# Running sums of a rotated attention trace from rounded high and low parts, with the context scaling moved to ScalarE

## What is computed

```python
v = x @ Wv.T
rotors = exp(1j * t[:, None] * freqs[None, :])
memory_trace = cumsum(v * rotors, axis=1)
retrieved = real(memory_trace * conj(rotors))
x = layernorm(x + retrieved @ Wo.T)

s = einsum('bsd,btd->bst', x, ctx) / 16 * Dm         # Dm: normalised decay, lower triangle
v = maximum(abs(sum(s, axis=-1)), 1.0)
x = layernorm(x + einsum('bst,btd->bsd', s / v[:, None, :], ctx))

logits = x @ router_w.T                               # top 2 of 8 experts, then the experts
x = layernorm(x + sum_e gate_e * (silu(x @ up_e) * (x @ up_e')) @ down_e)
```

## Time and profile before

| | us |
|---|---|
| median of three runs | 265.36 (264.54 to 266.08) |
| the profiled execution, own time | 262.09 |
| its span, first to last instruction | 260.3 |

### The profile page before, as it was taken

How to read it: one execution, slowest core, us unless ns; L and a number is a source line. 1 busy time by engine, 2 the same in 40 slices (tenths; PEclk the granted TensorE clock), 3 DMA queues, 4 the chain that set the end, 5 groups by cost and what they waited for, 6 DMA issues and landing times.

```text
span 260.3 us, 5161 instructions
## 1 busy us (share of the span) xinstructions
PE 206.9 (79%) x1365; PEld 181.5 (70%) x1366; DVE 162.7 (62%) x534; ACT 111.1 (43%) x277; POOL 143.0 (55%) x132
## 2 busy tenths in 40 slices
PE   8669899999999997756999999999999999300000
PEld 8557798898888996745888888888888888200000
DVE  5856888888887684954554544554545454118992
ACT  2323144244234113641454545454545454425665
POOL 0074674674675310565577777777777774416340
PEclk9999999999999999979999999999999999955555
DMA  7964665765641012802222323233232341089323
GB/s 217 383 260 149 239 188 197 231 229 184 225 122 43 0 44 89 276 3 60 81 89 92 101 86 101 89 99 101 85 101 89 102 91 66 9 271 317 139 90 151
DMA packets 20129, 35.73 MB, mean 137 GB/s; under 512 B 2861, under 2 KB 11312, under 8 KB 20112
## 3 DMA queue, kind: packets, MB, share of 16 engines
q1 hardware_dynamic: 16368, 26.21, 30.0%
q0 software_dynamic: 3744, 9.31, 11.8%
HBM read 27.12 MB, written 9.31 MB: 140 GB/s over the span
## 4 chain that ended last, share of the span: by engine, by line
PE 65%; DVE 17%; issue 6%; POOL 4%; DMA 4%; ACT 2%; SPq 1%; DVEq 0%; ACTq 0%; POOLq 0%
PE p_c L545 14%; PE p_v L545 7%; PE p_y L467 6%; PE p_v L411 4%; PE p_y L571 4%; PE p_r L545 4%; PE p_a L545 3%; PE p_s L545 3%; PE p_t L584 3%; PE p_s L451 3%; POOL space L992 3%; PE p_c L427 3%; DVE space L838 3%; PE p_r L495 2%; PE p_a L486 2%
## 5 line engine op out<-in xcount | busy, mean ns | idle before, releaser
L545 PE MATMUL p_c<-w_hi,parts 128*128 x104 | 34.7, 414 | 0.0
L1016 POOL DMA_INDIRECT y_dram<-x1T,scatter_now x26 | 26.3, 1013 | 11.8 <-issue 6.2
L996 POOL DMA_INDIRECT turns<-x_dram,gather_now x26 | 25.4, 979 | 12.6 <-issue 3.8
L983 POOL TENSOR_TENSOR w_lo<-keep,w_hi 128x1536 fp32r<-128x1536 f32 (+1 forms) x8 | 27.5, 3440 | 0.0
L810 DVE TENSOR_TENSOR parts<-p_y,parts 128x256 fp32r<-128x256 f32 x39 | 16.5, 424 | 17.4 <-ACT parts L912 17.4
L820 DVE TENSOR_TENSOR cs<-p_c,cs 128x256 f32<-128x256 f32 x26 | 11.0, 424 | 22.8 <-ACT cs L919 22.8
L970 POOL TENSOR_TENSOR space<-back 128x512 f32<-128x512 f32 x8 | 10.1, 1267 | 26.9 <-DVE back L704 26.9
L919 ACT ACTIVATE cs<-p_c 128x256 f32<-128x256 f32 x26 | 10.1, 387 | 24.8 <-PE p_c L545 24.8
L978 POOL TENSOR_TENSOR cs<-space,vinv 128x256 f32<-128x256 f32 x16 | 9.5, 613 | 18.3 <-DVE vinv L718 14.9
L545 PEld LDWEIGHTS p_c<-w_hi,parts 128*128 128x128 f32 x104 | 17.6, 189 | 2.4
L912 ACT ACTIVATE parts<-p_y 128x256 fp32r<-128x256 f32 x39 | 14.9, 381 | 8.6 <-PE p_y L571 8.5
(11 more groups left out here) (153 smaller groups left out, 551.4 us busy)
## 6 DMA issues: line engine op xcount, KB each, us to landing
keep<-in_weights SPq DMA_DIRECT2D x8, 768.0 KB, 4.4
space<-y_dram SPq DMA_DIRECT2D x16, 256.0 KB, 4.1
space<-in_xT SPq DMA_DIRECT2D x8, 256.0 KB, 3.5
keep<-in_x SPq DMA_DIRECT2D x8, 256.0 KB, 3.6
space<-in_ctxT SPq DMA_DIRECT2D x8, 256.0 KB, 2.8
space<-in_ctxt SPq DMA_DIRECT2D x8, 256.0 KB, 3.0
x_dram<-x SPq DMA_DIRECT2D x8, 256.0 KB, 2.2
keep<-x_dram SPq DMA_DIRECT2D x1, 2048.0 KB, 8.4
```

Of the source, the lines that this page charges most:

```text
L545: last = nc.tensor.matmul(dst, lhs[:, k, :], w[:].rearrange("p e n -> p (e n)")[:, bass.ds(start + col + k * width, width)], start=(n == 0 ...
L983: nc.gpsimd.tensor_tensor(w_lo[:, bass.ds(i, 1), :].rearrange("p a n -> p (a n)"), w_in[s], w_hi[:, bass.ds(i, 1), :].rearrange("p a n -> ...
L996: nc.gpsimd.indirect_dma_start(xs[s], None, x2_dram, bass.IndirectOffsetOnAxis(ap=gather_now[s][:], axis=0)).then_inc(xs_ok[s], 16)
L1016: nc.gpsimd.indirect_dma_start(y_dram, bass.IndirectOffsetOnAxis(ap=scatter_now[s][:], axis=0), ys[s], None, bounds_check=TOPK * N - 1, oo ...
```

## The change

Four things. (1) `turned` is split into `turned_hi`, its value rounded by ACT (two copies of 512 columns a pair), and `turned_lo`, the rest, subtracted by POOL (two of 512 columns); `tri` is copied once into the rounded `tri_exact`; the sums are now sixteen float32r matmuls, high and low part of each block adding into the same place of `p_c`. PE waits for the low part of each sequence by itself. (2) The context rows are no longer scaled; instead ACT scales `att` by `vinv` into `att_div` (two of 128 columns), and PE multiplies `att_div` by `c_in` directly. (3) ACT's `w_hi` stands right behind `sd1` instead of behind `vabs`, and POOL's `w_lo` is cut into four quarters of 384 columns, the first ahead of `got` and three behind it. (4) SP's load of the next context rows waits for the `p_a` matmuls, and its last read-back waits for `w_lo`.

```diff
--- before.py
+++ after.py
@@ -141,6 +141,7 @@
         att = sb("att", [P, 2, T])
+        att_div = sb("att_div", [P, 2, T])
@@ -161,6 +162,9 @@
         parts = sb("parts", [P, 4 * RING, KC, P], F32R)
+        turned_hi, turned_lo = (parts[:].rearrange("p a k t -> p (a k t)")[:, n * 4 * D:(n + 1) * 4 * D].rearrange(
+            "p (q h d) -> p q h d", q=2, h=2) for n in range(2))
+        tri_exact = sb("tri_exact", [P, P], F32R)
         shift = [sb(f"shift{s}", [P, 2]) for s in range(2)]
@@ -275,6 +279,7 @@
         eps_ok = sem("eps_ok")
+        tri_ok, turned_hi_ok, turned_lo_ok = (sem(n) for n in ("tri_ok", "turned_hi_ok", "turned_lo_ok"))
         v_ok, turned_ok, sums_ok, back_ok, got_ok, y_ok = (sem(n) for n in (
@@ -351,7 +356,7 @@
                     if has(-1):
-                        sp.wait_ge(cs_ok, i)
+                        sp.wait_ge(av_ok, i)
                     load(c_in, ctxt, c_ok, i + 1, 1 - s)
@@ -369,6 +374,8 @@
 
+            sp.wait_ge(lo_ok, PAIRS)
+
             sp.dma_start(x2_keep.rearrange("p j n -> p (j n)").rearrange("p (j q d) -> p (j q) d", q=2, d=D),
@@ -420,13 +427,16 @@
                 if has(0):
-                    pe.wait_ge(turned_ok, i + 1)
-                    for q in range(2):
+                    if isinstance(i, int) and i == 0:
+                        pe.wait_ge(tri_ok, 1)
+                    for q in range(2):
+                        pe.wait_ge(turned_lo_ok, 2 * i + q + 1)
                         for h in range(2):
                             for k in range(KC):
-                                last = nc.tensor.matmul(p_c[:, q, h, k * T:(k + 1) * T],
-                                                        turned[:, q, h, k * P:(k + 1) * P], tri,
-                                                        start=True, stop=True)
+                                for n, share in enumerate((turned_hi, turned_lo)):
+                                    last = nc.tensor.matmul(p_c[:, q, h, k * T:(k + 1) * T],
+                                                            share[:, q, h, k * P:(k + 1) * P], tri_exact[:],
+                                                            start=(n == 0), stop=(n == 1))
                     last.then_inc(sums_ok, 1)
@@ -438,7 +448,7 @@
                     if has(0):
-                        pe.wait_ge(turned_ok, i + 1)
+                        pe.wait_ge(turned_ok, 2 * i + 2)
                     values(0, xT_in[1 - s])
@@ -479,11 +489,12 @@
                     keep_busy(idle[3], ident, 0)
+                    pe.wait_ge(c_ok[1 - s], 8 * (i - 1 - (1 - s)) + 16)
                     pe.wait_ge(cs_ok, i)
...
                     for q in range(2):
-                        last = nc.tensor.matmul(p_a[:, q, :], att[:, q, :], cs[:, q, :], start=True, stop=True)
+                        last = nc.tensor.matmul(p_a[:, q, :], att_div[:, q, :], c_in[1 - s][:, q, :], start=True, stop=True)
                     last.then_inc(av_ok, 1)
@@ -654,10 +665,12 @@
                 dve.wait_ge(v_ok, j + 1)
+                if not (isinstance(j, int) and j == 0):
+                    dve.wait_ge(turned_lo_ok, 2 * j)
                 for q in range(2):
-                    last = nc.vector.tensor_tensor(
-                        turned[:, q, :, :], p_v[:, q:q + 1, :].to_broadcast([P, 2, D]), rotor[:, 0, :, :], ALU.mult)
-                last.then_inc(turned_ok, 1)
+                    nc.vector.tensor_tensor(
+                        turned[:, q, :, :], p_v[:, q:q + 1, :].to_broadcast([P, 2, D]), rotor[:, 0, :, :],
+                        ALU.mult).then_inc(turned_ok, 1)
 
@@ -867,23 +880,38 @@
             act.wait_ge(eps_ok, 1)
+            act.wait_ge(const_in, 16)
+            nc.scalar.activation(tri_exact[:], tri, ACT.Copy).then_inc(tri_ok, 1)
 
...
                     nc.scalar.activation(sd1[:], mv1[:, :, 1], ACT.Sqrt, bias=eps[:]).then_inc(sd1_ok, 1)
-                    act.wait_ge(t1_ok, i)
-                    nc.scalar.activation(x1T[:], p_t[:], ACT.Copy).then_inc(x1T_ok, 1)
-                if has(-2):
-                    act.wait_ge(mv2_ok, 2 * i - 2)
-                    nc.scalar.activation(sd2[:], mv2[:, :, 1], ACT.Sqrt, bias=eps[:]).then_inc(sd2_ok, 1)
-                if has(-1):
-                    act.wait_ge(sum_ok, i)
-                    nc.scalar.activation(vabs[:], rowsum, ACT.Abs).then_inc(vabs_ok, 1)
                 if has(0):
...
                                          ACT.Copy).then_inc(hi_ok, 1)
+                if has(-1):
+                    act.wait_ge(t1_ok, i)
+                    nc.scalar.activation(x1T[:], p_t[:], ACT.Copy).then_inc(x1T_ok, 1)
+                if has(-2):
+                    act.wait_ge(mv2_ok, 2 * i - 2)
+                    nc.scalar.activation(sd2[:], mv2[:, :, 1], ACT.Sqrt, bias=eps[:]).then_inc(sd2_ok, 1)
+                if has(-1):
+                    act.wait_ge(sum_ok, i)
+                    nc.scalar.activation(vabs[:], rowsum, ACT.Abs).then_inc(vabs_ok, 1)
+                    act.wait_ge(vinv_ok, i)
+                    if has(-2):
+                        act.wait_ge(av_ok, i - 1)
+                    for q in range(2):
+                        last = nc.scalar.activation(att_div[:, q, :], att[:, q, :], ACT.Copy, scale=vinv[:, q:q + 1])
+                    last.then_inc(cs_ok, 1)
+                if has(1):
+                    if has(0):
+                        act.wait_ge(sums_ok, i + 1)
+                    for q in range(2):
+                        act.wait_ge(turned_ok, 2 * i + 3 + q)
+                        nc.scalar.activation(turned_hi[:, q, :, :], turned[:, q, :, :], ACT.Copy).then_inc(turned_hi_ok, 1)
                 if has(-2):
@@ -962,28 +990,30 @@
 
+            def low_part(e, s, quarter):
+
+                n = slice(quarter * W_END // 4, (quarter + 1) * W_END // 4)
+                whole = w_hi[:, bass.ds(e, 1), :].rearrange("p a n -> p (a n)")
+                return nc.gpsimd.tensor_tensor(w_lo[:, bass.ds(e, 1), :].rearrange("p a n -> p (a n)")[:, n], w_in[s][:, n],
+                                               whole[:, n].bitcast(F32), ALU.subtract)
+
             def step(i, s, has):
                 if has(0):
+                    pool.wait_ge(hi_ok, i + 1)
+                    low_part(i, s, 0)
                     pool.wait_ge(back_ok, i + 1)
...
                                             back[:, :, 1, :].rearrange("p q (k t) -> p q k t", k=KC), ALU.add).then_inc(got_ok, 1)
-                if has(-1):
-                    pool.wait_ge(c_ok[1 - s], 8 * (i - 1 - (1 - s)) + 16)
-                    pool.wait_ge(vinv_ok, i)
-                    if has(-2):
-                        pool.wait_ge(av_ok, i - 1)
-                    for q in range(2):
-                        last = nc.gpsimd.tensor_tensor(cs[:, q, :], c_in[1 - s][:, q, :], vinv[:, q:q + 1].to_broadcast([P, D]), ALU.mult)
-                    last.then_inc(cs_ok, 1)
-
-                if has(0):
-                    pool.wait_ge(hi_ok, i + 1)
-                    nc.gpsimd.tensor_tensor(w_lo[:, bass.ds(i, 1), :].rearrange("p a n -> p (a n)"), w_in[s],
-                                            w_hi[:, bass.ds(i, 1), :].rearrange("p a n -> p (a n)").bitcast(F32),
-                                            ALU.subtract).then_inc(lo_ok, 1)
-
+                    for quarter in range(1, 4):
+                        last = low_part(i, s, quarter)
+                    last.then_inc(lo_ok, 1)
+                if has(1):
+                    for q in range(2):
+                        pool.wait_ge(turned_hi_ok, 2 * i + 3 + q)
+                        nc.gpsimd.tensor_tensor(turned_lo[:, q, :, :], turned[:, q, :, :],
+                                                turned_hi[:, q, :, :].bitcast(F32), ALU.subtract).then_inc(turned_lo_ok, 1)
             pipeline(pool, step)
```

More of the change, by code:

```diff
@@ L874, in step @@
                     nc.scalar.activation(sd1[:], mv1[:, :, 1], ACT.Sqrt, bias=eps[:]).then_inc(sd1_ok, 1)
+                if has(0):
+                    act.wait_ge(w_ok[s], 8 * (i - s) + 16)
+                    nc.scalar.activation(w_hi[:, bass.ds(i, 1), :].rearrange("p a n -> p (a n)"), w_in[s],
+                                         ACT.Copy).then_inc(hi_ok, 1)
+                if has(-1):
                     act.wait_ge(t1_ok, i)
@@ L882, in step @@
                     nc.scalar.activation(vabs[:], rowsum, ACT.Abs).then_inc(vabs_ok, 1)
-                if has(0):
-                    act.wait_ge(w_ok[s], 8 * (i - s) + 16)
-                    nc.scalar.activation(w_hi[:, bass.ds(i, 1), :].rearrange("p a n -> p (a n)"), w_in[s],
-                                         ACT.Copy).then_inc(hi_ok, 1)
+                    act.wait_ge(vinv_ok, i)
[5 more added lines that the diff above has]
+                if has(1):
+                    if has(0):
+                        act.wait_ge(sums_ok, i + 1)
+                    for q in range(2):
```

(2 more changed lines are left out.)

1 line of the change is left out of this document (removed).

## The result

The changed kernel takes **279.15 us** (277.99 to 280.55, four runs) against 264.95 for the kernel before in the same runs: ratio **1.057 [1.052, 1.063]**, 14.2 us slower. The forecast was 275.8, with a range of 270.5 to 281.5.

What follows compares the result with a forecast made beforehand. PE was taken to bound the middle, at about 9.65 us a step, and a chain of waits the start. Start +6.05, pair 1 +0.2, middle +4.5 and end -0.3 made +10.45: 275.8 us, range 270.5 to 281.5.

Steps and rivals of the forecast that it cites:

- The sign: Whole kernel: the change makes it slower, chance 0.96, against faster 0.03 and same 0.01.
- the sums: Sums on PE: sixteen rounded matmuls take 1.76 to 1.95 us in place of 1.89, nothing won or lost.
- the start: Pair 0: ACT rounds only behind its last Sin, then PE runs the sums at half clock, turn back at 17.9, +6.05.
- The rival in which they halve and PE keeps that: Sums on PE: they halve, saving 0.94 us in seven steps, total change -3.0, 262.4 us; chance 0.04.
- The 0.5 given back a step later: After pair 1's transposes: one step on, x1 is no longer under POOL's long w_lo, so 0.5 us returns.
- The middle: Steps 2 to 6: POOL's quarters hold DVE's x2, so x2T is late and PE stalls, 0.9 a step, +4.5.
- The step that failed: Middle, x2's normalisation: only the second quarter precedes the second L651, x2 at 53.5 instead of 52.87, vinv at 53.9.
- POOL runs all three quarters through: Middle: DVE gets in only after all three quarters, x2 at 54.6, 1.85 a step, +15.2, 280.5 us; chance 0.08.
- 0.15 a step for `att_div`: Middle, ACT: att_div at 0.4 us each pushes the rounding by 0.15, counted within the 0.9 a step.
- The rest costs nothing there: Middle: other moved work, such as w_hi ahead of x1T, POOL's subtractions and SP's context load, adds 0.
- The end: End of the stage: L682 is no longer slowed from 0.26 to 0.64 us by POOL's context scaling, -0.3.
- holding 0.2 to 1.85 a step: Middle: bounds on the loss per step from POOL's quarters holding DVE, 0.2 without holding, 1.85 with all three run through.

Runs made afterwards that it cites:

- the low part placed: Changed kernel with w_lo in two pieces, 640 columns behind vinv and 896 behind x1 of the next step: 267.45 us, ratio 1.0132.
- the placed scaling: Kernel before with only context scaling moved to ACT, w_hi at the start of the step and whole w_lo behind vinv: 261.73 us, ratio 0.9928.
- everything placed: Changed kernel with w_lo cut at column 640 into gaps, pair 0 rounded early, 24 idle matmuls at the start, x2T between the roundings: 264.83 us, ratio 1.0082.

## Why the prediction was right, and where it was not

**The sign, the sums and the start: right.** The sums came at 1.85 us (chain, 70.92), within 1.76 to 1.95, and the run with sixteen rounded matmuls shows the term of 0 by itself. The rival in which they halve and PE keeps that is refuted twice: sixteen take as long as before, and with eight, which do take half as long, the kernel is slower. The Trainium skill ("FP8 and Floating Point Precision", TensorE Precision Notes) gives true fp32 four passes; the one pass for the rounded form, and with it the 0.95 us for the sixteen, was an estimate from there, since the page puts no number to that form. Here 1.85 stands against it. The start was forecast at +6.05 with the turn back at 17.9 and came at 17.72, +5.86, step for step: roundings 11.93 to 13.06, sums from 14.03, half clock from 12. Pair 0's transposes were forecast at 26.6 and came at 26.68. The 0.5 given back a step later did not come (9.88 instead of 9.63), so pair 1 is 0.9 us later than said.

**The middle: right in kind, mis-sized.** The term was +4.5, 0.9 a step in five steps; it was 11.45. The step that failed is "The second quarter gets in before the second L651, to 53.4: x2 is ready at 53.5 ... Maximum and reciprocal take 0.38". What was wrong in it and beside it:
- After the quarters stands `vmax`, which I took to be free at 0.17. It is held for the third quarter, 0.96. The Trainium skill ("SBUF — State Buffer", Who interferes with whom) names `tensor_scalar` among the instructions that can take the shared ports, when its operands meet the conditions for that, and speaks of no size. This row, a `tensor_scalar` of 128x2 at 0.96, agrees. I had applied it to L651 and not to the small one behind it. In effect this is the price of the rival *POOL runs all three quarters through* (1.85 a step), by another way.
- A quarter took 1.00 us where I took 0.86, so three end 0.4 later.
- PE was forecast to wait ahead of the logits alone. It waits there (0.51), and already ahead of `p_a` (0.72), since `att_div` follows the late `vinv`. The chain runs through x2T, so this second wait shows the same delay and adds none.
- The clock falls in the middle, of which I had not spoken. One fall lay on the chain and cost 1.8 us (13.12 against 11.29); the other steps with half clock differ from those at full clock by 0.4 at most.

The bill of the middle: 1.64 - 0.74 for x2 and 0.96 - 0.17 for `vmax` are 1.69 us, and the step at full clock is 11.32 against 9.58, 1.74 more. Five such steps are 8.7, the fall 1.8, and 0.9 remains, most of it the sixth step (10.24 against 9.51). What I had counted on top, 0.15 a step for `att_div` and the wait of x2T behind the second rounding, is small: with the low part placed and ACT's order left as it is, steps are 9.56.

**"The rest costs nothing there": half right.** `w_hi` ahead of x1T is hidden, as said. Moving the scaling to ACT was also counted as free but for the 0.15, and by itself it costs 5.7 us, since what it delays is `w_lo`, which then holds x1 (and in one step the clock fell). In the change as it stands this doesn't show, since the change also moves `w_hi` and cuts `w_lo`.

**The end:** the term was -0.3 and it was -0.4.

**The sum.** Between the traces +18.5 against +10.45, between the medians +14.2. The value was inside the range for the medians, and that is in part luck: the range reached to 16.1 above the median before, and the trace of the kernel after, which is that of the longest of its four runs, lies 18.5 above the trace before. The middle came out 2.5 times as large as its term. The interval of causes that made the range (holding 0.2 to 1.85 a step) did contain the 1.74 that was measured.

**Left open.** Why PE's clock falls behind some short pauses and not behind others. Whether the gain of the placed scaling comes from the place of `w_lo` alone or also from the earlier `w_hi` was not tried apart, nor was the placed `w_lo` with the scaling left on POOL. In *everything placed* the shares of the early rounding, the fill and x2T's place were not separated.

## What to carry to other kernels

When a change gives POOL more elementwise work, or delays it, lay its instructions against DVE's in the timeline and list every DVE instruction under them, the small ones too: the cost is what these wait, it goes straight onto whatever chain they are in, and here, moving the POOL work into the gaps took back 11.7 of 14.2 us without removing any. A dent in TensorE's clock beside such a wait can be its follower; a few idle matmuls tell (the clock returned and the time stayed). And before halving a group on the busiest engine, look which chain has the same length beside it.

## What the runs showed of the hardware

- Held DVE instructions are not only the wide ones: a `tensor_scalar` of 128x2 took 0.96 us under a POOL subtraction against 0.17 free, and a `scalar_tensor_tensor` of 128x256 1.37 against 0.42. PSUM-reading additions and multiplications of the same step (0.66 to 0.69) stayed as they were.
- Float32r matmuls with 128 moving columns, two for one of fp32: 1.85 us for sixteen, 116 ns apart, against 118 for the 16 records of eight fp32 ones.
- Less work on TensorE brought its clock down and cost time: with eight matmuls of sums instead of sixteen the granted clock was 0.50 from 54 to 56 us, and three of the steps took 11.1 to 11.2, where with sixteen all took 9.5 to 9.9.
- Idle matmuls kept the clock at 1.00 in the middle and gained 0.1 us or less a step (11.38 against 11.46 over five); in the sixth they cost 0.9.
- Behind pauses of TensorE of about the same length the clock fell in one execution (2.26 us, then 0.50 from 12 to 16 us) and not in another (2.44 us, 1.00).
